# Two-layer graph kernel: zero rows held until the last step's sums are loaded, the last block summed behind the down products, message rows stored ahead of residual rows

## The reference

```python
xn = _layernorm(x)
x = x + _L0_gnn_ref(xn, src, dst, edge_weight, ...) + _L0_mix_ref(xn[None], ...)[0]
x = x + _L0_ffn_ref(_layernorm(x)[None], ...)[0]      # 8 experts, top 1
xn = _layernorm(x)
x = x + _L1_gnn_ref(xn, weight, bias, src, dst) + _L1_mix_ref(xn[None], ...)[0]
x = x + _L1_ffn_ref(_layernorm(x)[None], ...)[0]      # 8 experts, top 2
# the graph sum of layer 1
msg = (h * norm_src[:, None])[src]
agg = jax.ops.segment_sum(msg, dst, num_segments=n) * norm_dst[:, None]
out = jax.nn.elu(agg @ weight + bias)
# the mixer of layer 1 ends with
ff = jax.nn.relu(x @ W1 + b1) @ W2 + b2
x = _layernorm(x + ff, ln2_g, ln2_b)
```

## Time and profile before

| | us |
|---|---|
| median of 3 runs | 3760.94 (3758.91 to 3763.25) |
| the profiled execution | 3755.32 |
| its span, first to last instruction | 3753.6 |
| PE busy | 2703.4 (72%) |
| POOL busy | 2379.1 (63%) |
| DVE busy | 1099.5 (29%) |
| ACT busy | 494.6 (13%) |
| mean granted TensorE clock | 0.754 |

### The profile page before, as it was taken

How to read it: one execution, slowest core, us unless ns; L and a number is a source line. 1 busy time by engine, 2 the same in 40 slices (tenths; PEclk the granted TensorE clock), 3 DMA queues, 4 the chain that set the end, 5 groups by cost and what they waited for, 6 DMA issues and landing times.

```text
span 3753.6 us, 36443 instructions
## 1 busy us (share of the span) xinstructions
PE 2703.4 (72%) x9839; PEld 1997.6 (53%) x9840; DVE 1099.5 (29%) x3529; ACT 494.6 (13%) x1086; POOL 2379.1 (63%) x1962
## 2 busy tenths in 40 slices
PE   0689796796797885599548767767686786755786
PEld 0355575574575674388425445545464454434665
DVE  4444433313233322100223323433333323321000
ACT  0112010010010100233211101101110010102222
POOL 0678887887788875122148788878787787732444
PEclk9889776676676676699758777767686676667889
DMA  3544533433333434222253353434333343342333
GB/s 104 136 125 126 153 98 82 109 88 88 101 86 94 108 82 113 67 64 65 74 158 102 94 145 86 119 78 110 92 93 106 86 113 91 84 118 41 80 69 55
DMA packets 354903, 364.43 MB, mean 97 GB/s; under 512 B 203633, under 2 KB 282412, under 8 KB 354783
## 3 DMA queue, kind: packets, MB, share of 16 engines
q0 software_dynamic: 270976, 270.76, 29.5%
q1 hardware_dynamic: 77307, 86.00, 7.3%
q10 hardware_dynamic: 6500, 6.41, 0.6%
HBM read 291.95 MB, written 71.28 MB: 97 GB/s over the span
## 4 chain that ended last, share of the span: by engine, by line
POOL 23%; PE 9%; issue 8%; another core or an unknown queue 4%; DMA 3%; DVE 2%; POOLq 1%; SPq 1%; ACT 0%; DVEq 0%; ACTq 0%
POOL xg L541 21%; PE bank L645 8%; DMA xg<-feat,idx_cur 2%; POOL sorted_in L597 1%; PE bank L651 1%; DMA feat<-arena 1%; POOL xg L547 0%; DMA out_rows<-arena,ids_cur 0%; POOLq L532 0%; DVE arena L1229 0%; SPq L447 0%; DVE oh L1351 0%; SPq L450 0%; DVE bn L1212 0%
## 5 line engine op out<-in xcount | busy, mean ns | idle before, releaser
L541 POOL DMA_INDIRECT xg<-feat,idx_cur x1600 | 1970.3, 1231 | 569.9 <-issue 433.9
L645 PE MATMUL bank<-xg,oh 125*125 125x256 f32 (+1 forms) x3324 | 1085.9, 482 | 533.3 <-DMA xg<-feat,idx_cur 431.2
L645 PEld LDWEIGHTS bank<-xg,oh 125*125 125x125 f32 x3324 | 738.3, 234 | 856.6 <-DMA xg<-feat,idx_cur 606.2
L651 PE MATMUL bank<-ident,arena 125*128 125x125 f32 x700 | 174.8, 381 | 352.4 <-remote 237.0
L645 PE MATMUL bank<-t,w_h 128*128 128x250 f32 (+1 forms) x1184 | 329.7, 432 | 14.7 <-remote 8.0
L651 PEld LDWEIGHTS bank<-ident,arena 125*128 125x128 f32 x700 | 104.5, 190 | 421.4 <-issue 419.0
L1351 DVE TENSOR_SCALAR oh<-iota,dst_cur 125x125 f32<-125x125 f32 x800 | 190.1, 354 | 425.2 <-PE bank L645 415.5
L645 PEld LDWEIGHTS bank<-t,w_h 128*128 128x128 f32 x1184 | 231.9, 201 | 110.0 <-issue 58.9
L1348 DVE TENSOR_SCALAR oh<-iota,dst_cur,w_cur 125x125 f32<-125x125 f32 x800 | 232.2, 430 | 131.5 <-PE bank L645 121.3
L645 PE MATMUL bank<-w_exp,arena 128*125 128x256 f32 x1024 | 253.2, 408 | 0.0
L645 PE MATMUL bank<-arena 125*125 125x25 bf16 (+2 forms) x1000 | 230.9, 390 | 17.2 <-DVE arena L1488 17.2
(11 more groups left out here) (255 smaller groups left out, 2239.3 us busy)
## 6 DMA issues: line engine op xcount, KB each, us to landing
xg<-feat,idx_cur POOLq DMA_INDIRECT x1600
sorted_in<-pad_rows POOLq DMA_DIRECT2D x16, 878.4 KB, 17.9
arena<-sorted_in SPq DMA_DIRECT2D x49, 251.0 KB
arena<-rows_b SPq DMA_DIRECT2D x5, 1875.0 KB
w_exp<-in_L_ffn_Wd POOLq DMA_DIRECT2D x8, 1024.0 KB
w_exp<-in_L_ffn_W POOLq DMA_DIRECT2D x16, 512.0 KB
arena<-in_x SPq DMA_DIRECT2D x10, 625.0 KB
feat<-arena SPq DMA_DIRECT2D x10, 625.0 KB
```

What stands on the lines that cost most here:

```text
L541: pool.indirect_dma_start(xg[:, s, 0:D], None, feat, bass.IndirectOffsetOnAxis(ap=idx_cur[g % 2][:, s:s + 1], axis=0)).then_inc(xg_full[s ...
L645: return pe.matmul(o, w, r, start=first, stop=last, skip_group_check=not check)
L651: return pe.transpose(ps[:, at:at + n], src, ident[0:n, 0:n])
```

## The change

There are three edits. Neither arithmetic nor data change; only the order does.

1. In SP's queue between the layers the message rows of each step go ahead of its residual rows. The residual rows of steps 3 and 4 go as one transfer of 1280 KB behind the last message rows. nodes_stored now counts 32 in place of 48.
2. ends() is called inside the last step: in the first layer behind DVE's wait for the loaded sums (rowa_in) and the release of PE, in the second behind the wait for aggs_in.
3. In the plan LAST the last block (24) moves from "hidden", behind the hidden products, to a new stage "sums", which stands behind the down products on PE, behind the second norm's root on ACT, and behind the second norm and the residual add on DVE. ACT's step_ready follows it there.

```diff
-LAST = {"heads": ((0, ALL),), "norm": ((1, ALL),), "hidden": ((2, ALL),)}
+LAST = {"heads": ((0, ALL),), "norm": ((1, ALL),), "sums": ((2, ALL),)}
...
             for s in range(NS):
-                sp.wait_ge(nodes_full, s + 1)
-                sp.dma_start(rows(rows_b[:, 0:D], s), h_big[:, G * s:G * s + G, :]).then_inc(
-                    head_stored if s < 3 else nodes_stored, 16)
                 sp.wait_ge(msg_full, s + 1)
                 sp.dma_start(rows(feat1, s), msg[s % 2]).then_inc(msg_stored[s % 2], 16)
+                if s < 3:
+                    sp.dma_start(rows(rows_b[:, 0:D], s), h_big[:, G * s:G * s + G, :]).then_inc(head_stored, 16)
+            sp.dma_start(rows_b[3 * G * B:, 0:D].rearrange("(i p) d -> p i d", p=B), h_big[:, 3 * G:, :]).then_inc(
+                nodes_stored, 16)
...
                     last.then_inc(y_dve[i % 2], 1)
+                beside("sums", b, plan)
...
                 beside("hidden", b, plan)
-                step_ready()
+                if plan is MID:
+                    step_ready()
                 root(sd[:, :])
+                beside("sums", b, plan)
+                if plan is LAST:
+                    step_ready()
...
                 dve.sem_inc(v_full, 1)
+                if not more:
+                    ends()
...
-            ends()
             layer0(NS - 1, 0)
...
-            dve.wait_ge(nodes_stored, 48)
+            dve.wait_ge(nodes_stored, 32)
...
                 dve.sem_inc(rowb_used, 1)
+                beside("sums", b, plan)
...
                 take(dve, aggs_in, 16)
-
+                if plan is LAST:
+                    ends()
...
-            ends()
             mixer(NB - NL, LAST)
```

More of the change, by code:

```diff
@@ L1504, in positions @@
                 dve.sem_inc(pos_full, 1)
[L1506 to L1510, removed]
             def routes():
@@ L1527, in routes, with ends @@
                 dve.sem_inc(routes_full, 1)
+            def ends():
+                chain(dve.tensor_copy(tail_tab[:, :], cnt[0:1, :]))
+                dve.sem_inc(tails_known, 1)
+                chain.restart()
             def experts(layer):
```

## The result

| | before | after |
|---|---|---|
| median, us | 3759.93 (3758.45 to 3763.25, 4 runs) | 3729.83 (3727.29 to 3732.06, 4 runs) |
| the profiled execution | 3755.32 | 3732.06 |
| its span | 3753.6 | 3730.4 |

What follows compares the result with a forecast made beforehand. POOL's gathers were taken to bound the kernel, with the stretches before the first and behind the last gather of a layer; 10.6 + 15.1 + 8.2 = 33.9 us off 3760.9 gave 3727, range 3714 to 3743.

Steps and rivals of the forecast that it cites:

- the new wait: Second layer's last step: held zero rows land at 3388.3, 16 us after the positions, and the scatter waits for them.
- the second layer's term: Second layer's last step: the scatter, 3396.54 before, starts at 3388.3, a gain of 8.2 us, 0.2 at worst.
- The first two terms: Message rows ahead between the layers, 10.6 us, and zero rows held in the first layer's last step, 15.1 us.
- Message rows first: Between the layers: message rows ahead in SP's queue move POOL's first gather two slots earlier, 10.6 us.
- The slots: SP's queue between the layers: landings come some 5.3 us apart; message 4 moves from slot 10 to slot 8.
- Rival 2: Between the layers: message order gives nothing, since the chain of norms, not the slots, sets m4; median 3738; 9%.
- First layer: Last step: with zero rows held, the load takes 7.6 instead of 22.9 us, gaining 15.1; lower bound 10.1.
- Second layer, sums: Last step: store lands in 3.5 us, load takes 7.6, so sums are loaded 23.7 us earlier, at 3327.2.
- Second layer, zero rows: Last step: zero rows start at 3328.2, take 60.1 us, land at 3388.3; the scatter then starts, gaining 8.2 us.
- Rival 1: Second layer: POOL's pause after five zero-row transfers goes; zero rows take 51.8 us, gain 16.5, median 3718; 10%.
- Rival 3: Both last steps: zero rows only double a transfer, the rest being slow of itself; median 3749; 6%.
- Rival 4: Second layer: held zero rows become last while sums come no earlier; scatter slips 18 us; 3768; 4%.

Runs made afterwards that it cites:

- the second measurement: The changed kernel again with nothing altered, on one chip beside the one without the second layer's edits, against the kernel before: ratio 0.9933, -27.9 us.

## Why the prediction was right, and one term too large

3727 was forecast, 3729.83 measured. The direction, the place of each gain and the new wait came as written; the sum was 33.9 us against 30.1 by the medians, and 27.9 in the second measurement. What fell short was the second layer's term. The first two terms, 25.7 us together, came as 26.7 in the kernel that has only them.

- **Message rows first: 10.6 us forecast, 10.6 measured** in the stretch (85.21 to 74.64). The slots held: message 4 was to be computed from 1895.6 to 1897.8 of the old clock, which is 59.3 us behind L444; it was done at 59.3 (1884.26 + 2.10 - 1827.04). Rival 2, that the norms set its time, is out. In the kernel with this edit alone the whole time moved by 6.3 us with an interval up to 10.5; the trace and the interval touch, no more, and its gathers took 1382.8 us, so they did not give the gain back.
- **First layer: 15.1 forecast, 14.2 measured from store to PE's turn** (load to PE -14.7, store to load +0.4). The wait of the scatter stayed covered, with 6 us to spare instead of 9. The 7.6 us taken for a load alone came from one with four more behind it in the queue; the first layer's loads with the zero rows held took 8.2 to 8.6. Behind PE's turn came 2.4 us more that no term had. One us of it is a small DVE instruction on the path that took 1.15 us while POOL was issuing its last three zero rows, and 0.17 now (below). Another us is luck: PE's 80 gate products took 13.91 us before, 12.87 after and 15.81 in the second execution of the changed kernel, with the granted clock falling from 1.00 to 0.50 about 3.3, 4.5 and 1.3 us into them. PE, timeline, in this order:

```profile
1527.91 13.91 PE L645 MATMUL bank<-wg,arena 128*125 128x8 f32 x80 [0.97 <-remote]
1516.29 12.87 PE L646 MATMUL bank<-wg,arena 128*125 128x8 f32 x80 [0.97 <-remote]
1514.35 15.81 PE L646 MATMUL bank<-wg,arena 128*125 128x8 f32 x80 [0.97 <-remote]
```

  From PE's turn to the scatter it was 73.1, 70.7 and 73.7 us in the three: behind PE's turn the second execution gained nothing. Over all executions this stretch took 71.9 to 75.1 us in the kernels that don't hold the zero rows and 70.5 to 73.7 in those that do.
- **Second layer, sums: right.** Edit 3 left the last store where it was forecast, 25.7 us earlier with the rest (3290.3; it came at 3291.23). The store's wait went from 22.3 to 3.1 us (forecast 3.5), the load from 12.6 to 8.0 us up to the cast (forecast 7.6), so the sums came 23.8 us earlier, where 23.7 stood in the sum.
- **Second layer, zero rows: the step that was mis-sized.** The prediction let them start 1 us behind the sums and take 60.1 us; they started 1.9 us behind the cast and took 65.7. So 0.9 us was left of the 8.2, inside the bound of 0.2 but far from the value taken. In the second execution of the same kernel they took 59.0, and 7.4 us were left. In the whole time the second layer's edits gave 2.8 us without the others and 1.2 us on top of them, neither told from zero, where 8.2 stood. The prediction had two values for this length, 60.1 and 63.1, one per layer of the one profiled execution, took the lower and did not ask how far one execution can be from another: in the second layer of the executions here it ran from 58.1 to 65.7 us. A term that is the difference of two long times (the 68 us from the release of the zero rows to the scatter's old start, less their own 60) has the whole spread of the longer one in it.
- **Rival 1**, POOL's pause gone when its queue begins empty, did not come: the pause was 33.3 us and 26.9. The mechanism is nevertheless that of the prediction's remark: the last three are issued when the fifth has landed (42.8 and 36.3 us from the start in the two executions; the sixth issued at 43.3 and 36.8). With 502 KB each there is no such pause.
- **Rival 3**, that zero rows only double a transfer beside them: fell. The store's wait went down by a factor of 7 and the first layer's load by 2.8, to about what a load takes alone; the second layer's load, down by 1.6, would have fitted it. The other rule that the prediction took from the Trainium skill, DMA: Bandwidth & Descriptors, Queues, rings and completion order (a semaphore's increment lands only behind every earlier write of the same DMA engine), gives the whole wait back, and 22.3 to 3.1 us agrees with it in size. The packets in the traces don't support it as the cause. ACT's queue carries the store as 130 packets. Before, the first of them is seen 3 us behind the issue, 110 were done by 3328, and the other 20, 0.02 MB, came singly among the zero rows' packets up to 3337.5, five with 0.01 MB of data in the microsecond from 3336; SP issued the load at 3338.30. After, all 130 ran from 3292.0 to 3293.6, and the load was issued at 3294.36. So both times the load came 0.8 us behind the last packet: the wait lay in the packets themselves, and not in an increment that came late behind them. The other four traces with zero rows released ahead of the store show the same, with the last packet at most about a us ahead of the load. Why single packets of a small transfer come so late stays open. In the first layer the store, issued 1 us ahead of the zero rows, was through in 3.5 us; there the load, issued behind them, took the 22.9 us.
- **Rival 4**, slower, came for edit 2 without edit 3, where the release is late because DVE is still in its norm: +13.0 us. In the changed kernel the order of edit 3 keeps that from happening.

Why the fifth zero-row transfer landed at 42.8 us in one execution and 36.3 in another was not settled.

## What to carry to other kernels

A bulk write that nobody waits for soon is not free: ask which small transfer follows it in time, and what stands behind that one. Holding it back pays only if its own length fits under what remains, so before moving it late, look for a place where it can run early; here writing the same zero rows from another queue some 180 us sooner was worth more than all of the second layer's edits. And when two edits each remove one of two waits that end together, try them together as well as alone: alone they gave +13.0 and +0.9 us, together -2.8 with an interval that takes in zero, and with the zero rows out of the way edit 3 alone was worth about 17.

## What the runs showed of the hardware beside that

**How much POOL can have queued.** With transfers of 878 KB POOL stopped after five (4.4 MB) in every execution and layer where it issued them, for 26 to 33 us, until the fifth had landed. With 502 KB it issued all eight (4.0 MB) within 17.4 us, with gaps of 0.2 to 2.1 us. So it isn't the number of DMAs alone; whether the amount or the number of rows counts wasn't tried. Nor is it simply what is under way: with 878 KB the first transfer had landed after 8.5 to 9.9 us, and POOL still issued nothing until the fifth had. SP, given the same eight of 878 KB, was held by the issues themselves for 71.3 us.

**A small DVE instruction beside POOL's issues.** The DVE instruction on the way to PE's next turn in the first layer, in the trace of before and of after:

```profile
1495.36 1.15 DVE L1225 TENSOR_SCALAR sd<-mv 125x5 f32<-125x5 f32 x1
```
```profile
1485.00 0.17 DVE L1231 TENSOR_SCALAR sd<-mv 125x5 f32<-125x5 f32 x1
```

It took 1.15, 1.41, 0.74 and 0.84 us in four of the executions in which POOL was issuing its last three zero rows at that moment (1492.8 to 1498.4 before), and 0.17 in the seven in which POOL was doing nothing. In one (block 24 moved, alone) POOL was issuing as well and it took 0.17. PE sat idle 7.9 to 9.7 us before its next turn in the four where this was slow (8.33 before), and 7.35 or 7.36 in the eight where it wasn't. That POOL's issuing is the cause is not shown by an experiment of its own.

**PE's clock behind that idle time.** PE sits idle while DVE norms, and its granted clock falls from 1.00 (2.4 GHz) to 0.50 (1.2 GHz). Windows of before and after (last three columns: clock, DMA share, GB/s):

```profile
1495.00:1500.00 5.00, 0.00 (x0) 0.00 (x0) 3.13 (x12) 1.49 (x2) 3.38 (x2) 0.71 0.67 182
1500.00:1505.00 5.00, 3.11 (x11) 1.60 (x11) 0.24 (x1) 1.90 (x5) 0.00 (x0) 0.50 0.71 159
1510.00:1515.00 5.00, 5.00 (x16) 3.04 (x16) 0.00 (x0) 1.79 (x4) 0.00 (x0) 0.93 0.43 116
```
```profile
1485.00:1490.00 5.00, 0.77 (x4) 0.70 (x4) 2.06 (x7) 1.49 (x2) 0.00 (x0) 0.66 0.77 138
1490.00:1495.00 5.00, 3.58 (x10) 1.71 (x9) 0.00 (x0) 1.90 (x5) 0.00 (x0) 0.50 0.71 157
1495.00:1500.00 5.00, 3.90 (x11) 2.28 (x10) 0.00 (x0) 2.22 (x3) 0.00 (x0) 0.82 0.60 166
```

Before, it stayed at the lower level for some 13.6 us (from the mean 0.71 the fall is at 1497.1, from 0.93 the rise at 1510.7), after for some 10.2 (1486.6 to 1496.8, from 0.66 and 0.82). In all twelve executions this stay was either 10.2 us (eight) or 13.6 to 13.7 (four), and it doesn't follow the slow DVE instruction: with block 24 moved alone the instruction took 0.17 us and the stay was 13.6, with the second layer's zero rows held alone it took 0.84 and the stay was 10.2. Here the longer stay cost little: from PE's turn behind the norm to its gate products it was 27.3 us before and 27.1 after. The fall of the clock that costs more is the next one, in the gate products.
